# Products of probabilities and values issued once per group, at unit 6, in place of twice, at units 2 and 6

## What is computed

```python
qkv = (x @ qkv_w.T + qkv_b).reshape(B, T, 3, H, dh)
scores = jnp.einsum('bhtd,bhsd->bhts', q, k) * scale
scores = jnp.where(causal, -jnp.inf, scores)
attn = jax.nn.softmax(scores, axis=-1)
seq_out = jnp.einsum('bhts,bhsd->bhtd', attn, v)
...
x = _layernorm(x + _L0_attn_ref(...))
x = _layernorm(x + _L0_ffn_ref(...))
```

## Time and profile before

| | us |
|---|---|
| median of 3 runs | 818.73 |
| lowest, highest | 816.57, 823.24 |
| the profiled execution | 814.79 |
| its span, first to last instruction | 813.1 |

### The profile page before, as it was taken

How to read it: one execution, slowest core, us unless ns; L and a number is a source line. 1 busy time by engine, 2 the same in 40 slices (tenths; PEclk the granted TensorE clock), 3 DMA queues, 4 the chain that set the end, 5 groups by cost and what they waited for, 6 DMA issues and landing times.

```text
span 813.1 us, 12395 instructions
## 1 busy us (share of the span) xinstructions
PE 717.8 (88%) x4004; PEld 498.5 (61%) x4004; DVE 604.8 (74%) x2105; ACT 350.6 (43%) x701; POOL 423.9 (52%) x334
## 2 busy tenths in 40 slices
PE   5994998999898999998989988879999899999995
PEld 2552665666565666665656654547777677676774
DVE  2254777778888889898898777637778777887685
ACT  2311555555455556555546556723233242342411
POOL 9300994997676776776675971514315043151310
PEclk9995999999999999999999986889999999999998
DMA  7899599674574756756655745031130321303000
GB/s 278 255 246 174 134 139 149 168 123 101 136 108 98 164 79 145 143 93 146 127 75 144 125 101 183 2 103 47 33 104 1 104 68 37 104 1 104 27 27 26
DMA packets 60420, 89.88 MB, mean 111 GB/s; under 512 B 8234, under 2 KB 37316, under 8 KB 60356
## 3 DMA queue, kind: packets, MB, share of 16 engines
q1 hardware_dynamic: 60356, 89.09, 48.8%
HBM read 54.72 MB, written 33.82 MB: 109 GB/s over the span
## 4 chain that ended last, share of the span: by engine, by line
PE 48%; DVE 27%; DMA 8%; ACT 6%; issue 5%; POOL 4%; SPq 2%; ACTq 0%; DVEq 0%; POOLq 0%
PE ps L1257 15%; PE ps L374 8%; PE ps L338 6%; PE ps L327 6%; DVE ps L469 6%; DMA Q<-MT 6%; PE ps L315 5%; DVE Ob L517 4%; DVE A L1391 3%; PE ps L232 2%; ACT X L1243 2%; PE ps L1222 2%; ACT Pr L412 1%; DVE Z L1277 1%; DVE HL L478 1%
## 5 line engine op out<-in xcount | busy, mean ns | idle before, releaser
L469 DVE CUSTOM_DVE_ANT_0 ps<-ps,mask 128x256 f32<-128x256 f32 (+3 forms) x512 | 237.3, 510 | 39.3 <-PE ps L315 38.9
L412 ACT ACTIVATE Pr<-ps 128x512 f32<-128x512 f32 (+2 forms) x384 | 189.9, 528 | 129.0 <-PE ps L327 124.3
L327 PE MATMUL ps<-Q,K 98*128 98x256 f32 (+2 forms) x512 | 174.3, 383 | 28.8 <-DMA Q<-MT 18.6
L1257 PE MATMUL ps<-ew_hi,XT 128*128 128x512 f32 x512 | 176.6, 403 | 0.0
L315 PE MATMUL ps<-K,Q 96*128 96x256 f32 (+2 forms) x512 | 154.2, 347 | 21.7 <-DVE nmax L469 21.2
L1391 DVE SCALAR_TENSOR_TENSOR A<-ps,cw,A 128x256 f32<-128x256 f32 x256 | 123.7, 483 | 47.0 <-PE ps L1257 34.5
L327 PEld LDWEIGHTS ps<-Q,K 98*128 98x128 f32 x512 | 93.3, 196 | 83.1 <-issue 27.9
L613 POOL TENSOR_SCALAR_AFFINE_SELECT Pr<-Pr 128x512 f32<-128x512 f32 x128 | 89.4, 715 | 90.4 <-ACT Pr L412 87.8
L315 PEld LDWEIGHTS ps<-K,Q 96*128 96x128 f32 x512 | 101.0, 200 | 41.4 <-DVE nmax L469 27.6
L1257 PEld LDWEIGHTS ps<-ew_hi,XT 128*128 128x128 f32 x512 | 97.3, 190 | 21.3 <-issue 0.3
L1257 PE MATMUL ps<-ew_rest,XT 128*128 128x512 f32 x256 | 101.6, 397 | 0.0
(11 more groups left out here) (190 smaller groups left out, 1070.4 us busy)
## 6 DMA issues: line engine op xcount, KB each, us to landing
qk_scratch<-HL SPq DMA_DIRECT2D x32, 512.0 KB, 3.2
Q<-qk_scratch SPq DMA_DIRECT2D x96, 128.0 KB, 4.3
K<-qk_scratch SPq DMA_DIRECT2D x96, 128.0 KB, 5.8
Pr<-xT SPq DMA_DIRECT2D x8, 512.0 KB, 6.9
xraw<-xT SPq DMA_DIRECT2D x8, 512.0 KB, 6.5
mem_scratch<-Rl SPq DMA_DIRECT2D x16, 256.0 KB, 7.1
mv_scratch<-MV SPq DMA_DIRECT2D x32, 128.0 KB, 2.7
Wm<-mem_scratch SPq DMA_DIRECT2D x16, 256.0 KB, 9.1
```

The lines of the kernel that those rows point to most:

```text
L327: last = nc.tensor.matmul(o, K[0:STACK + 2, hh, P * kt:P * kt + P], Q[0:STACK + 2, hh, T - n:T], start=True, stop=True)
L412: nc.scalar.activation(probs(g % 2, kt, heads[0], len(heads)), src, ACT.Exp, scale=SCALE).then_inc(s_exp, 1)
L469: last = nc.vector.tensor_tensor_reduce(out=scores, in0=scores, in1=mask[:, T - w:T], scale=1.0, scalar=NEG, op0=ALU.add, op1=ALU.max, acc ...
L1257: last = nc.tensor.matmul(o, lhs(c, k), rhs(d, k), start=first, stop=(k == KT - 1 and c == 1))
```

## The change

`pe_batch` calls `pe_values` for key blocks 0 to 3 behind unit 6. Before, it called it for blocks 0 and 1 behind unit 2 and for 2 and 3 behind unit 6. The other engines' programs are the same, and so is what is computed. The first group of the kernel has no group before it and is not touched; the products of the very last group stand behind the loop and are not touched either.

```diff
@@ -386,8 +386,8 @@
                     on, ng, nu = ahead(g, u)
                     if not (last and on):
                         pe_max_scores(pe, b + on, ng, nu)
-                    if u in (2, 6) and not (first and g == 0):
-                        for kt in ((0, 1) if u == 2 else (2, 3)):
+                    if u == 6 and not (first and g == 0):
+                        for kt in range(QT):
                             pe_values(pe, pb, pg, kt)
                     if u in (4, 10) and not last:
                         pe_project(pe, b + 1, 2 * g + u // 10)
```

## The result

| | before | after |
|---|---|---|
| median of 4 runs, us | 817.65 | 846.43 |
| lowest, highest | 816.20, 823.24 | 842.53, 848.85 |
| span of the profiled execution | 813.1 | 847.1 |
| mean granted clock of TensorE | 0.951 | 0.935 |

The kernel became 3.2% slower: ratio 1.032, interval 1.027 to 1.038, 28.8 us. The forecast was a gain of 5.3 us. The time lies beyond the range, and beyond the worst rival's 832.6 as well. The two profiled executions are 34.0 us apart, 5.2 more than the medians: the one before was among the faster of its kernel, the one after the slowest of its four.

The account below looks back on a forecast made before the run. TensorE (51 of 55 us busy) and VectorE (49) were both near their limit, neither at it alone. Sum: 46.5 - 14.0 - 28.8 - 9.0 = -5.3 us, so 813.4 for the median; own range 809 to 818, overall 801 to 823.

Parts of the forecast that it names:

- the worst rival: Slower by the clock: waits at units 0 to 4 bring half clock behind them; 832.6 us, chance 0.20.
- The merge: Unit 6: one piece of 1280 columns takes 2.28 us in place of 0.78, +1.50 a group, +46.5 over 31.
- its cover: Units 7 to 9, behind the unit 6 piece: the addition falls into TensorE's waits for VectorE in fourteen groups, -14.0 us.
- the DMA: Unit 0: waits for the maxima's rows, brought by DMA, shrink by up to 1.50 us each, -9.0; bounds 4.5 and 10.5.
- Removed at units 0 to 4: Taking the unit 2 piece out gains, by what sets the pace in each kind of group, -28.8 us together.
- The light groups: Four groups with 0.88 to 1.13 us of VectorE idle behind the unit 2 piece: removal gains 1.45 each, 5.8.
- the eight groups: Units 0 to 4, VectorE idle 0.27 to 0.71: gain between 0.56 and 1.45 us, middle 1.0 taken, 8.0 together.
- The first groups of the batches: Six groups with scans at units 0, 2 and 4: removal gains 0.2 us each, 1.2 together, bounds 0 and 1.45.
- 13 groups: Groups where VectorE paces units 0 to 4: six with scans gain 1.2 us, seven more 2.2; same bounds, 0 and 1.45.
- The clock: Half clock behind waits at units 2 and 4; no term in the sum, only a rival with chance 0.20.
- Rival 3: Slower, clock: projection +1.10 us, merged piece at half clock +2.1, 3.2 a group; six groups give 832.6; chance 0.20.
- G29: Last batch, units 6 to 8 wait for expert weights' DMA whatever stands before; 1.5 us removed so its addition cancels.

Follow-up runs that it names:

- the addition alone: Kernel before, with unit 2's piece kept and unit 6 computing all four key blocks, so blocks 0 and 1 are done twice: 841.32 us, ratio 1.030.
- the removal alone: Kernel before, with the unit 2 piece (key blocks 0 and 1) left out in 31 groups, blocks 2 and 3 kept at unit 6: 825.73 us, ratio 1.011.
- the filled first groups: Kernel after, with eight useless matmuls at unit 2 of the first group of each batch only (seven times): 838.23 us, ratio 1.023.

## Why the prediction was wrong

*The merge, +1.50 at unit 6: right.* 2.28 us in the light group, +40.0 over 26 pieces where 39.0 was forecast.

*Added with its cover and the DMA, +23.5: right as a sum, and that in part by luck.* The run with the addition alone gave +23.4. Two of its terms were too large: in the trace of the kernel after the cover at units 7 to 9 was 9.6 us over the 26 intervals against 14.0 over 31 groups, and the waits for the rows of maxima shrank by 6.3 against 9.0; in the trace with the addition alone they are 9.7 and 6.4. The cover had been read from waits of weight loads, which run partly beside matmuls: in G13 these waits are 1.31 us, and units 7 to 10 shrank by 0.74. What made up for it was not in the sum: with the addition alone units 0 to 4 gave 3.3 us, and the projection at unit 10 with the turn 1.2.

*Removed at units 0 to 4, -28.8: the step that failed.* Its parts gave -14.7 over 26 intervals, and +8.0 in the projection behind it and +4.0 ahead of the piece took nearly all of that back; the run with the removal alone gave +7.8. The light groups were right: 1.56, 1.37 and 1.34 against 1.45. In the seventeen intervals of no clear kind 0.6 was won on average, where the middle of the bounds for the eight groups had 1.0. The first groups of the batches were given about nothing, with bounds at zero and 1.45, never below zero, and six of them came out 3.6 us worse than nothing. I wrote that VectorE paces 13 groups at units 0 to 4, which means that A cost nothing there; from that alone no gain could come, and the lower bound had no right to stop at zero. A loss could, and did.

*The clock, priced at zero in the sum: the second failure, of the same step.* Rival 3 had named the mechanism, its place (waits at units 2 to 4, then the projection) and its price of 1.10, which is the price seen (2.54 against 1.39 in the earlier trace rows). Among the 195 longest pieces of the chain there are 3 projections over 2.1 us before, 9 after, 16 with the removal alone and 1 with the addition alone. It was wrong in its second price: outside the last batch no merged piece ran wholly at half clock (three of 26 took 2.67, 2.50 and 2.57, the others 2.28), so the time was not reached by six groups at 3.2. In three of six first groups it is about 1.1 for the projection plus 1.50 for the longer piece with nothing won at unit 2, in the other three the piece alone, with 0.6 ahead of it and 0.7 at units 0 to 4 in one of them. The other 4.6 us of the +8.0 are projections in later groups of a batch.

"TensorE: Matmul & The Clock Gate", HAM oscillation, of the Trainium skill describes matmul bursts that start slow behind a wait for a DMA. In this case the wait is for VectorE, 1.90 us behind one of 0.70, and the trace agrees in kind. The page gives no price for so short a wait.

*The last batch, not set apart: wrong by 9.* I let G29 cancel and left the others in the general sum. But the piece at unit 6 of G30 stands in front of the way into the last part, and behind it TensorE waits 2.93 us and goes on at half clock. Two merged pieces of that batch run below full clock (3.06 and 4.33 us against 2.28), where three A pieces did before.

*The sum.* TensorE's busy share of 51 in 55 us was read as a claim on the time. The run without A shows that it was none. The Trainium skill's "Perfetto Trace Analysis", Identifying Performance Opportunities, says to improve the engine with the highest occupancy, though it warns against matmul busy time as the measure; in this case 54 us less work on the busiest engine gave +7.8 us.

**What stays open.** No run sets the clock by itself: that the useless matmuls act through it is an exclusion, with the granted clock of the traces and the projection's 1.68 against 2.56 behind it. The clock's share is an estimate, at most 12.0 of the 22.7 us in the 26 intervals. Where the 8.2 us of the filled first groups lie is not known. The 0.4 us in each of the other 21 groups is a remainder. Why unit 3 is already worse than unit 2 for blocks 0 and 1 (5.1 us) was not looked into. In the last batch the addition alone gives 4.2 of the 8.1 us without half clock at the piece; the rest was not taken apart.

## What to carry to other kernels

Before you count work taken off an engine as a gain, ask who sets the pace where it stands: where another engine does, the work is free, its removal is worth nothing, and its new place must be paid in full. The bounds for a removal should reach below zero if the engine is TensorE and it waits longer in the gap: in this kernel the projection behind the gap then took up to 2.56 us in place of 1.68. Leaving the piece out, and separately doing it twice, splits such a change into its two terms, and the trace of before held the answer to one of them only.

## What the runs showed of the hardware

Useless matmuls can make a kernel faster: with A left out, 28 us of them took 6.0 us off (825.73 to 819.71), and half clock was granted for 54.6 us in place of 88.7 over the same 26 intervals. Another 13 us in seven gaps took 8.2 us off the kernel after (846.43 to 838.23). A wait of TensorE of 1.90 us behind one of 0.70 was followed by a projection at half clock, and one of 1.04 behind A, or of 1.03 behind eight full-clock matmuls, was not. Two pieces of column-strip products a unit apart cost 0.31 us more than one of the same columns. And a wait of a weight load is not yet time on the path: 1.31 us of such waits in one group were worth 0.74.
